# Three accumulation banks in attention and one buffer set in the quantization of a two-layer transformer kernel

## The chip, the cores and the metric

The kernel runs on 8 cores of one Trainium2 chip. Each core works on one of 8 sequences (2048 tokens by 1024 features), all with the same program and without exchange between them. The metric is the time on the device of the slowest core, in microseconds (us).

## The reference, cut to what matters

Two transformer layers, each an attention and a feed-forward block on a layer-normalized input, each added to x. All data is float32.

```python
x = x + L0_attn(layernorm(x))     # 16 heads of 64; causal; low-rank q, k, v; RMS norms on q and k
x = x + L0_ffn(layernorm(x))      # 1024 x 1024, ternary weights, activations rounded to 8 bits
x = x + L1_attn(layernorm(x))     # 16 heads of 64; causal; latent k and v
x = x + L1_ffn(layernorm(x))      # 1024 -> 4096 -> 1024

def L0_ffn(x, weight):
    w_scale = mean(abs(weight)) + 1e-8
    w_quant = clip(round(weight / w_scale), -1, 1)
    a_scale = max(abs(x), axis=-1, keepdims=True) + 1e-8
    a_quant = round(clip(x / a_scale * 127.0, -128.0, 127.0))
    return einsum('bsi,oi->bso', a_quant, w_quant) * (w_scale * a_scale / 127.0)
```

## The kernel before

**Stages.** x stays on the chip, transposed: eight tiles `X[c]` of 128 features by 2048 tokens. The stages follow one another with a barrier between them: entry (transposes), layer-0 attention `emit_l0a`, layer-0 feed-forward `emit_l0f`, layer-1 attention `emit_l1a`, layer-1 feed-forward, exit. The token axis is cut into four windows `qq` of 512 (`QW`).

**How the order comes about.** Every instruction is written by `do(engine, build, r=..., w=...)`. The five engines' queues run in the order in which the calls are written. From the names that an instruction reads (`r`) and writes (`w`) the helper works out what it waits for: a reader for the last writer of the name, a writer for the last writer and all readers. There are no other waits within a stage.

**Attention.** `attn_head` computes one head, in both layers, window by window. A window of queries has 4, 8, 12 or 16 blocks of 128 keys. Per block: the scores (L334, in the banks PS0, 1, 4 and 5 in turn), on the diagonal a mask added by a second matmul (L340), the exponential on ScalarE (L346, three tiles E32 in turn), and two blocks later the product with V (L352), which accumulates over the window in the bank `pvb`. That bank is PS2 in windows 0 and 2 and PS3 in windows 1 and 3. At the window's end ScalarE forms the reciprocal of the sums (L385 reads the bank, L388). The window's epilogue is held back and written after the fourth block of the next window, or at the start of the next pair of heads: TensorE moves the reciprocal to the other half of the partitions (L359, bank PS6), VectorE copies it (L363), multiplies the bank by it (L366, the last reader of the bank) and adds into X (L370). There are 2 layers of 8 pairs of heads, 4 windows a head, 128 windows in all. Ahead of each pair of heads TensorE makes its projections; in layer 0 they use the banks PS0 to PS7 (those of V, L627, PS2 and PS3; the norm sums PS6 and PS7), in layer 1 the banks PS2 to PS5, PS2 first. A prologue in layer 1 uses PS7 once.

**Quantization, in `emit_l0f`.** For each window the scale is spread over the partitions (L877, copied by L881 to RAB), and then for each of the eight chunks c of 128 features:
- GpSimd: XN = (X - MU) (L313), times RBC (L317), times RAB (L892);
- ScalarE: U = XN + 128.5 (L897), R = U (L901);
- VectorE, for k = 7 down to 0: B = (R >= 2^k) * 2^k (L906), R = R - B (L910), which leaves the fraction in R; then AQW[c] = U - 128 - R (L913), the rounded value.

The tiles XN, U, R and B are there twice and are taken in turn (in the trace `U__95`, `R__97`, `B__99`, `XN__101` are one set, `U`, `R`, `B`, `XN` the other). The matrix product L923 follows: eight output blocks of eight matmuls, each first block's matmul waiting for its chunk of AQW. VectorE scales each block's result (L938) and GpSimd adds it into X (L941); after that the next window begins.

Of the kernel before, what the change touches and what calls it, by code (L numbers as in the profile page):

```python
# [7 lines left out]
F32 = mybir.dt.float32  # L8
BF16 = mybir.dt.bfloat16
AF = mybir.ActivationFunctionType  # L10
OP = mybir.AluOpType
# [4 lines left out]
NCH = 8  # L16
NQ = 4
QW = 512
# [14 lines left out]
class KB:  # L33
# [286 lines left out]
    def attn_head(self, k_lhsT, kkey, q_rhs, qkey, v_lhsT, vkey, negc, nkey,  # L320
                  xout, xkey, half):
        s = self
        hs_ctx = slice(64, 128) if half else slice(0, 64)
        hs_z = slice(0, 64) if half else slice(64, 128)
        for qq in range(NQ):
            kcmax = 4 * qq + 4
            pvb = 2 + (qq % 2)
# [52 lines left out]
            if kcmax >= 2:  # L380
# [5 lines left out]
                 r=(f"PS{pvb}",), w=("TMPK",))  # L386
# [3 lines left out]
                 r=("TMPK",), w=("RBFz",))  # L390
# [293 lines left out]
    def emit_l0f(self):  # L684
        s = self
        WQ = s.ov("WQB", [128, 8 * 1024], BF16, 0)
        AQW = s.ov("AQW", [128, 8 * QW], BF16, 16 * 1024)
# [7 lines left out]
        UP = [s.ov("U_", [128, QW], F32, 62 * 1024),  # L695
              s.ov("U2", [128, QW], F32, 100 * 1024)]
        RP = [s.ov("R_", [128, QW], F32, 94 * 1024),
              s.ov("R2", [128, QW], F32, 102 * 1024)]
        BP = [s.ov("B_", [128, QW], F32, 96 * 1024),
              s.ov("B2", [128, QW], F32, 24 * 1024)]  # L700
        XNP = [s.ov("XN_", [128, QW], F32, 98 * 1024),
               s.ov("XN2", [128, QW], F32, 26 * 1024)]
        U_ = UP[0]
        XN_ = XNP[0]
# [16 lines left out]
        for m in range(2):  # L721
            for ch in range(8):
# [9 lines left out]
                 r=("PS2",), w=(f"AT{m}",))  # L732
# [142 lines left out]
        for qq in range(NQ):  # L875
# [6 lines left out]
            for c in range(NCH):  # L882
                p = (qq * NCH + c) % 2
                Ut, Rt, Bt, XNt = UP[p], RP[p], BP[p], XNP[p]
                uk, rk, bk_, xk = f"Up{p}", f"Rp{p}", f"Bp{p}", f"XNp{p}"
                wx = ("XN00", "XN01", "XN02", "XN03") if qq == 0 and c == 0 \
                    else ()
                if qq == 0 and c == 1:
                    wx = ("WPB",)
                s.xn_into(XNt[:], xk, c, qq, eng="gpsimd", wx=wx)  # L890
                s.do("gpsimd", lambda e, XNt=XNt, RAB=RAB:
                     e.tensor_tensor(XNt[:], XNt[:], RAB[:], OP.mult),  # L892
                     r=(xk, "RAB"), w=(xk,))
                uwx = ("XN10", "XN11", "XN12", "XN13") if qq == 0 and c == 0 \
                    else ()
                s.do("scalar", lambda e, Ut=Ut, XNt=XNt:
                     e.activation(Ut[:], XNt[:], AF.Identity,  # L897
                                  bias=s.SM[:, 30:31], scale=1.0),
                     r=(xk, "SM30"), w=(uk,) + uwx)
                s.do("scalar", lambda e, Rt=Rt, Ut=Ut:  # L900
                     e.activation(Rt[:], Ut[:], AF.Copy), r=(uk,), w=(rk,))  # L901
                for k in range(7, -1, -1):
                    val = float(1 << k)
                    kwx = ("WPB",) if qq == 0 and c == 1 and k == 7 else ()
                    s.do("vector", lambda e, val=val, Bt=Bt, Rt=Rt:
                         e.tensor_scalar(Bt[:], Rt[:], val, val, OP.is_ge,  # L906
                                         OP.mult),
                         r=(rk,), w=(bk_,) + kwx)
                    s.do("vector", lambda e, Rt=Rt, Bt=Bt:
                         e.tensor_tensor(Rt[:], Rt[:], Bt[:], OP.subtract),  # L910
                         r=(rk, bk_), w=(rk,))
                s.do("vector", lambda e, c=c, Ut=Ut, Rt=Rt, AQW=AQW:
                     e.scalar_tensor_tensor(  # L913
                         AQW[:, QW * c:QW * (c + 1)],
                         Ut[:], -128.0, Rt[:], OP.add, OP.subtract),
                     r=(uk, rk), w=(f"AQc{c}",))
# [580 lines left out]
```

How the kernel before makes its waits and increments, by code:

```python
        def f(e, build=build, real=tuple(real), sn_inc=sn_inc, n=n):  # L99
            for (sn, v0) in real:
                e.wait_ge(sems[sn], v0)
            build(e).then_inc(sems[sn_inc], n)
# [19 lines left out]
    def barrier(self):  # L122
        self.flush_ep()
        self.do("sync", lambda e: e.nop(),
                xw=[(sn, self.cnt[sn]) for sn in (*self.LDS, *self.STS)])
        vals = {}
        for e in ENGS:
            vals[e] = self.do(e, lambda en: en.nop(),
                              xw=[(ESEM[e], self.cnt[ESEM[e]])], force=True)
        for e in ENGS:
            for o in ENGS:
                if o == e:
                    continue
                sn = ESEM[o]
                if self.hw[e].get(sn, 0) < vals[o]:
                    self.hw[e][sn] = vals[o]
                    self.th[e].append(
                        lambda en, sn=sn, v0=vals[o]: en.wait_ge(self.sems[sn], v0))
            for sn in (*self.LDS, *self.STS):
                self.hw[e][sn] = max(self.hw[e].get(sn, 0), self.cnt[sn])
        self.floor = {ESEM[o]: vals[o] for o in ENGS}
        for sn in (*self.LDS, *self.STS):
            self.floor[sn] = self.cnt[sn]
```

## Time and profile before

| what | us |
|---|---|
| median of the timed runs (2) | 8110.35 |
| the two runs | 8074.76 and 8145.95 |
| the profiled execution | 7631.25 |
| its span on the slowest core | 7629.7 |
| spans of the eight cores | 7614.0 to 7629.7 |

Busy time in the profiled execution, on the slowest core:

| engine | busy us | share of the span | instructions |
|---|---|---|---|
| TensorE, matmuls (PE) | 5883.9 | 77% | 15346 |
| VectorE (DVE) | 2305.8 | 30% | 3740 |
| ScalarE (ACT) | 2055.3 | 27% | 3076 |
| GpSimd (POOL) | 618.5 | 8% | 580 |

The profile is of one execution, so durations and spans are to be compared with its own time and not with the median. Shares over the whole span are averages over stages that differ. "PEclk" is the granted TensorE clock as a share of 2.4 GHz. "Idle before" is time in which the engine stood still ahead of an instruction, put down to what released it last.

### The profile page before, as it was taken

Reading aid. Unit: us, or ns where it says so; the run is one execution under the profiler, and the core shown is the slowest. Engines: PE = TensorE matmul, PEld = TensorE weight load, DVE = VectorE, ACT = ScalarE, POOL = GpSimd, SP = SyncE. Lnnn points to the kernel's source line nnn. Section 1 sums busy time; section 2 is a strip of 40 time slices with the busy share of each in tenths; the row PEclk is TensorE's granted clock in tenths of the full one; section 3 lists DMA queues with packets and bytes.
Section 4 is the critical chain, followed back from the end, with each engine's and each line's share of the span. In section 5 each row is a group of like instructions: output and inputs, shape, how many; then the busy total and the mean of one; then the engine's idle time right before and its main releaser. Section 6 shows DMA issues by size and latency. Waiting matters only on the chain.

```text
span 7629.7 us, 101825 instructions; the slowest of 8 cores (7614.0 to 7629.7 us)
## 1 busy us (share of the span) xinstructions
PE 5883.9 (77%) x15346; PEld 2147.1 (28%) x15346; DVE 2305.8 (30%) x3740; ACT 2055.3 (27%) x3076; POOL 618.5 (8%) x580
## 2 busy tenths in 40 slices
PE   6888988889863112769878988898678879789786
PEld 2333333333321000222222222223223323223232
DVE  1333223332204677121111111111233332342323
ACT  1333333333310000103222322232342341432420
POOL 0000000000002332000000000000020120210200
PEclk8888998889975555889889989898889989999896
DMA  1000000000011000000000000000022222122221
GB/s 54 1 1 1 1 1 1 1 1 1 1 39 50 1 0 0 17 1 1 1 7 1 1 1 1 1 1 1 12 62 73 67 62 84 56 67 73 62 73 67
DMA packets 58437, 179.44 MB, mean 24 GB/s; under 512 B 9723, under 2 KB 16294, under 8 KB 57894
## 3 DMA queue, kind: packets, MB, share of 16 engines
q1 hardware_dynamic: 57894, 172.92, 7.4%
q8 instruction: 253, 4.15, 0.2%
q14 instruction: 290, 2.38, 0.1%
HBM read 164.44 MB, written 8.39 MB: 23 GB/s over the span
## 4 chain that ended last, share of the span: by engine, by line
PE 68%; DVE 15%; issue 8%; ACT 4%; DMA 2%; POOL 1%; DVEq 1%; ACTq 0%; SPq 0%; POOLq 0%; PEldq 0%
PE PS L334 16%; PE PS L352 15%; PE PS L1316 11%; PE PS L1252 7%; PE PS L340 2%; DVE W1L L1218 2%; PE PS L359 2%; ACT W1H L1216 1%; PE PS L279 1%; DVE R__97 L910 1%; PE PS L274 1%; DVE R L910 1%; PE PS L1001 1%; PE PS L1016 1%; PE PS L961 1%
## 5 line engine op out<-in xcount | busy, mean ns | idle before, releaser
L346 ACT ACTIVATE E<-PS,SM 128x512 f32<-128x512 f32 x1280 | 864.2, 686 | 1362.1 <-PE PS L340 684.4
L363 DVE COPY RBF<-PS 64x512 f32<-64x512 f32 x128 | 88.2, 689 | 2253.3 <-PE PS L359 2183.9
L334 PE MATMUL PS<-QP,KHD 64*128 64x512 f32 x1280 | 746.7, 675 | 10.8 <-issue 10.6
L352 PE MATMUL PS<-E,VFB 128*128 128x512 f32 x1280 | 659.7, 611 | 4.6 <-ACT E L346 4.6
L352 PE MATMUL PS<-E,VFA 128*128 128x512 f32 x1280 | 656.6, 611 | 1.3 <-ACT E L346 1.3
L1252 PE MATMUL PS<-XNH,W1H 128*128 128x512 bf16 x1024 | 434.9, 425 | 186.3 <-ACT W1H L1216 147.5
L1252 PE MATMUL PS<-XNH,W1L 128*128 128x512 bf16 x1024 | 436.2, 426 | 122.5 <-DVE W1L L1218 107.0
L1284 POOL TENSOR_TENSOR SC<-SC 128x512 f32<-128x512 f32 x128 | 161.6, 1263 | 3484.9 <-PE PS L1252 3454.1
L1252 PE MATMUL PS<-XNL,W1H 128*128 128x512 bf16 x1024 | 430.2, 420 | 0.3 <-DVE XNL L1200 0.2
L923 PE MATMUL PS<-AQW,WQB 128*128 128x512 bf16 x256 | 78.0, 445 | 455.8 <-DVE AQW L913 444.9
L1316 PE MATMUL PS<-ACH,W1H 128*128 128x512 bf16 x1024 | 388.8, 380 | 34.6 <-ACT ACH L1295 34.4
L1316 PE MATMUL PS<-ACL,W1H 128*128 128x512 bf16 x1024 | 388.8, 380 | 9.5 <-POOL ACL L1302 4.2
L1316 PE MATMUL PS<-ACH,W1L 128*128 128x512 bf16 x1024 | 388.7, 380 | 0.2
L334 PE MATMUL PS<-QA,KA 128*128 128x512 f32 x640 | 338.2, 623 | 0.0
L334 PEld LDWEIGHTS PS<-QP,KHD 64*128 64x128 f32 x1280 | 204.8, 196 | 471.7 <-issue 469.2
L1236 DVE TENSOR_TENSOR W1L<-W2F,W1H 128x1024 bf16<-128x1024 f32 x128 | 157.3, 1229 | 585.2 <-PE PS L1316 543.8
L334 PE MATMUL PS<-QB,KB 128*128 128x512 f32 x640 | 321.5, 596 | 0.0
L1233 ACT ACTIVATE W1H<-W2F 128x1024 bf16<-128x1024 f32 x128 | 135.1, 1055 | 671.7 <-PE PS L1316 671.7
L352 PEld LDWEIGHTS PS<-E,VFB 128*128 128x128 f32 x1280 | 231.2, 192 | 297.0 <-issue 290.7
L352 PEld LDWEIGHTS PS<-E,VFA 128*128 128x128 f32 x1280 | 232.3, 192 | 290.7 <-issue 284.3
L1218 DVE TENSOR_TENSOR W1L<-W1F,W1H 128x1024 bf16<-128x1024 f32 x127 | 177.2, 1395 | 316.5 <-ACT W1H L1216 267.1
L404 ACT ACTIVATE SC<-SC 128x2 f32<-128x2 f32 x32 | 6.5, 203 | 848.9 <-DVE SC L400 848.7
(243 smaller groups left out, 6823.6 us busy)
## 6 DMA issues: line engine op xcount, KB each, us to landing
W1F<-w1p SPq DMA_DIRECT2D x128, 512.0 KB, 3.7
W2F<-w SPq DMA_DIRECT2D x128, 512.0 KB, 3.6
TM<-x_in SPq DMA_DIRECT2D x16, 512.0 KB, 12.2
WTR<-w0T SPq DMA_DIRECT2D x16, 512.0 KB, 3.8
y_out<-XO SPq DMA_DIRECT2D x16, 512.0 KB, 2.6
WPA<-wo1T SPq DMA_DIRECT2D x16, 256.0 KB, 2.6
WPA<-wuq SPq DMA_DIRECT2D x8, 128.0 KB, 2.0
WPB<-wuk SPq DMA_DIRECT2D x8, 128.0 KB, 2.0
```

Of the source, the lines that this page charges most:

```text
L334: e.matmul(s.PS[sb][:], k_lhsT(kc), q_rhs(qq), start=True, stop=not diag),
L340: e.matmul(s.PS[sb][:], s.I128B[:], s.MSK[:, QW * j:QW * (j + 1)], start=False, stop=True),
L346: e.activation(s.E32[eb][:], s.PS[sb][:], AF.Exp, bias=negc),
L352: e.matmul(pvbank[:], v_lhsT(kc), s.E32[eb][:], start=(kc == 0), stop=(kc == kcmax - 1)),
L359: e.matmul(s.PS[6][hs_ctx, :], s.I128[hs_z, hs_z], s.RBF[hs_z, :], start=True, stop=True),
L910: e.tensor_tensor(Rt[:], Rt[:], Bt[:], OP.subtract),
L1218: e.tensor_tensor(w1l[:], w1f[:], w1h[:], OP.subtract),
L1233: e.activation(w2h[:, 0:1024], w2f[:], AF.Copy),
L1236: e.tensor_tensor(w2l[:, 0:1024], w2f[:], w2h[:, 0:1024], OP.subtract),
L1252: e.matmul(bank[:], lh[:, FCW * kc:FCW * (kc + 1)], rh[:, QW * kc:QW * (kc + 1)], start=(kc == 0 and pi == 0), stop=(kc == 7 and pi == 2)),
L1284: e.tensor_tensor(s.SC[0][:], s.SC[0][:], s.SC[3][:], OP.add),
L1316: e.matmul(s.PS[mch][:], lh[:, 128 * mch:128 * (mch + 1)], rh[:, QW * kc:QW * (kc + 1)], start=(kc == 0 and pi == 0), stop=(kc == 31 and p ...
```

## The change

Two edits. In `attn_head` the accumulation bank is taken from three, PS2, PS3 and PS7, by a counter that runs on over windows, heads and layers. In `emit_l0f` the second set of the tiles U, R, B and XN is dropped, and every chunk uses the one set under one set of names; the instructions themselves stay the same in kind, size, number and order.

```diff
         for qq in range(NQ):
             kcmax = 4 * qq + 4
-            pvb = 2 + (qq % 2)
+            s.pvc = getattr(s, "pvc", 0) + 1
+            pvb = (2, 3, 7)[s.pvc % 3]
             pvbank = s.PS[pvb]
...
-        UP = [s.ov("U_", [128, QW], F32, 62 * 1024),
-              s.ov("U2", [128, QW], F32, 100 * 1024)]
-        RP = [s.ov("R_", [128, QW], F32, 94 * 1024),
-              s.ov("R2", [128, QW], F32, 102 * 1024)]
-        BP = [s.ov("B_", [128, QW], F32, 96 * 1024),
-              s.ov("B2", [128, QW], F32, 24 * 1024)]
-        XNP = [s.ov("XN_", [128, QW], F32, 98 * 1024),
-               s.ov("XN2", [128, QW], F32, 26 * 1024)]
-        U_ = UP[0]
-        XN_ = XNP[0]
+        U_ = s.ov("U_", [128, QW], F32, 62 * 1024)
...
             for c in range(NCH):
-                p = (qq * NCH + c) % 2
-                Ut, Rt, Bt, XNt = UP[p], RP[p], BP[p], XNP[p]
-                uk, rk, bk_, xk = f"Up{p}", f"Rp{p}", f"Bp{p}", f"XNp{p}"
...
-                s.xn_into(XNt[:], xk, c, qq, eng="gpsimd", wx=wx)
+                s.xn_into(XN_[:], "XN", c, qq, eng="gpsimd", wx=wx)
...
-                s.do("scalar", lambda e, Ut=Ut, XNt=XNt:
-                     e.activation(Ut[:], XNt[:], AF.Identity,
+                s.do("scalar", lambda e, U_=U_, XN_=XN_:
+                     e.activation(U_[:], XN_[:], AF.Identity,
                                   bias=s.SM[:, 30:31], scale=1.0),
-                     r=(xk, "SM30"), w=(uk,) + uwx)
-                s.do("scalar", lambda e, Rt=Rt, Ut=Ut:
-                     e.activation(Rt[:], Ut[:], AF.Copy), r=(uk,), w=(rk,))
+                     r=("XN", "SM30"), w=("U",) + uwx)
+                s.do("scalar", lambda e, R_=R_, U_=U_:
+                     e.activation(R_[:], U_[:], AF.Copy), r=("U",), w=("R",))
                 for k in range(7, -1, -1):
                     val = float(1 << k)
...
-                         r=(rk,), w=(bk_,) + kwx)
+                         r=("R",), w=("B",))
...
-                         r=(rk, bk_), w=(rk,))
+                         r=("R", "B"), w=("R",))
...
-                     r=(uk, rk), w=(f"AQc{c}",))
+                     r=("U", "R"), w=(f"AQc{c}",))
```

## Rows read from the trace of the kernel before

**Rows 1.** Busy time by stage (from:to, length, engines' busy us, granted clock, DMA).
```profile
1000.00:2030.00 1030.00, 923.34 (x2108) 360.33 (x2107) 311.00 (x521) 376.12 (x581) 36.08 (x28) 0.89 0.00 1
...
2500.00:2900.00 400.00, 51.65 (x146) 16.35 (x146) 296.51 (x431) 32.44 (x48) 113.51 (x87) 0.53 0.00 0
...
3435.00:5380.00 1945.00, 1722.40 (x3648) 564.33 (x3647) 294.87 (x582) 555.56 (x831) 0.00 (x0) 0.90 0.00 1
...
5500.00:7520.00 2020.00, 1689.62 (x6124) 615.51 (x6122) 690.18 (x912) 634.36 (x895) 309.35 (x256) 0.92 0.22 67
```

**Rows 2.** TensorE's waits, whole run: line, releaser, us, times, longest.
```profile
PE PS L923 <- DVE AQW L913: 444.9, 31, 26.2
...
PE PS L352 <- ACT E L346: 5.9, 17, 1.3
...
PE PS L627 <- DVE TMPE L366: 2.9, 4, 0.9
```

**Rows 3.** Timeline over a border between heads: start, us, engine, line, operation.
```profile
363.83 1.07 PE L359 MATMUL PS<-RBF,I 64*64 64x512 f32 x2
...
365.94 0.68 DVE L366 TENSOR_TENSOR TMPE<-PS,RBF 64x512 f32<-64x512 f32 x1 [0.17 <-DVE RBF L363]
...
369.78 1.10 PE L352 MATMUL PS<-E,VFB 128*128 128x512 f32 x2 [0.39 <-ACT E L346]
```

**Rows 4.** Groups of the quantization, 2500 to 3060: count, busy, mean ns, idle before.
```profile
L910 DVE TENSOR_TENSOR R__97<-R__97,B__99 128x512 f32<-128x512 f32 x128 | 110.2, 861 | 13.3
...
L906 DVE TENSOR_SCALAR B__99<-R__97 128x512 f32<-128x512 f32 x128 | 81.4, 636 | 37.4 <-ACT R__97 L901 19.5 <-POOL XN L892 6.0
...
L897 ACT ACTIVATE U__95<-XN__101,SM 128x512 f32<-128x512 f32 x16 | 11.5, 722 | 617.9 <-POOL XN__101 L892 457.0 <-DVE AQW L913 160.9
```

**Rows 5.** Timeline of the first chunk of window 1.
```profile
2657.40 0.72 ACT L897 ACTIVATE U__95<-XN__101,SM 128x512 f32<-128x512 f32 x1 [47.79 <-POOL XN__101 L892]
2658.26 0.63 ACT L901 ACTIVATE R__97<-U__95 128x512 f32<-128x512 f32 x1
...
2659.07 1.10 DVE L906 TENSOR_SCALAR B__99<-R__97 128x512 f32<-128x512 f32 x1 [6.49 <-ACT R__97 L901]
...
2669.67 1.69 DVE L910 TENSOR_TENSOR R__97<-R__97,B__99 128x512 f32<-128x512 f32 x1
```

**Rows 6.** Timeline of the handover from that chunk to the next.
```profile
2676.85 0.69 DVE L913 SCALAR_TENSOR_TENSOR AQW<-U__95,R__97 128x512 bf16<-128x512 f32 x1 [0.17 <-DVE R__97 L910]
2677.46 0.42 DVE L906 TENSOR_SCALAR B<-R 128x512 f32<-128x512 f32 x1
2677.69 0.72 ACT L897 ACTIVATE U__95<-XN__101,SM 128x512 f32<-128x512 f32 x1 [14.58 <-DVE AQW L913]
...
2678.56 0.63 ACT L901 ACTIVATE R__97<-U__95 128x512 f32<-128x512 f32 x1
2678.61 1.27 POOL L313 TENSOR_TENSOR XN__101<-X,MU 128x512 f32<-128x512 f32 x1 [7.81 <-ACT U__95 L897]
2678.78 1.38 DVE L906 TENSOR_SCALAR B<-R 128x512 f32<-128x512 f32 x1
...
2680.27 1.63 DVE L910 TENSOR_TENSOR R<-R,B 128x512 f32<-128x512 f32 x1
2681.61 1.40 POOL L892 TENSOR_TENSOR XN__101<-XN__101,RAB 128x512 f32<-128x512 f32 x1 [0.27 <-POOL XN__101 L317]
...
2683.40 0.69 DVE L910 TENSOR_TENSOR R<-R,B 128x512 f32<-128x512 f32 x1
...
2690.91 0.69 DVE L913 SCALAR_TENSOR_TENSOR AQW<-U,R 128x512 bf16<-128x512 f32 x1 [0.17 <-DVE R L910]
```

**Rows 7.** VectorE's timeline: the last instruction of later chunks of window 1.
```profile
2733.11 0.69 DVE L913 SCALAR_TENSOR_TENSOR AQW<-U__95,R__97 128x512 bf16<-128x512 f32 x1 [0.17 <-DVE R__97 L910]
...
2744.41 0.69 DVE L913 SCALAR_TENSOR_TENSOR AQW<-U,R 128x512 bf16<-128x512 f32 x1 [0.17 <-DVE R L910]
...
2767.01 0.69 DVE L913 SCALAR_TENSOR_TENSOR AQW<-U,R 128x512 bf16<-128x512 f32 x1 [0.17 <-DVE R L910]
```

More of the change, by code:

```diff
@@ L882, in emit_l0f @@
             for c in range(NCH):
-                p = (qq * NCH + c) % 2
-                Ut, Rt, Bt, XNt = UP[p], RP[p], BP[p], XNP[p]
-                uk, rk, bk_, xk = f"Up{p}", f"Rp{p}", f"Bp{p}", f"XNp{p}"
                 wx = ("XN00", "XN01", "XN02", "XN03") if qq == 0 and c == 0 \
                     else ()
-                if qq == 0 and c == 1:
-                    wx = ("WPB",)
-                s.xn_into(XNt[:], xk, c, qq, eng="gpsimd", wx=wx)
-                s.do("gpsimd", lambda e, XNt=XNt, RAB=RAB:
-                     e.tensor_tensor(XNt[:], XNt[:], RAB[:], OP.mult),
-                     r=(xk, "RAB"), w=(xk,))
+                s.xn_into(XN_[:], "XN", c, qq, eng="gpsimd", wx=wx)
@@ L894, in emit_l0f @@
+                s.do("gpsimd", lambda e, XN_=XN_, RAB=RAB:
+                     e.tensor_tensor(XN_[:], XN_[:], RAB[:], OP.mult),
+                     r=("XN", "RAB"), w=("XN",))
                 uwx = ("XN10", "XN11", "XN12", "XN13") if qq == 0 and c == 0 \
                     else ()
-                s.do("scalar", lambda e, Ut=Ut, XNt=XNt:
-                     e.activation(Ut[:], XNt[:], AF.Identity,
+                s.do("scalar", lambda e, U_=U_, XN_=XN_:
+                     e.activation(U_[:], XN_[:], AF.Identity,
@@ L898, in emit_l0f @@
                                   bias=s.SM[:, 30:31], scale=1.0),
-                     r=(xk, "SM30"), w=(uk,) + uwx)
-                s.do("scalar", lambda e, Rt=Rt, Ut=Ut:
-                     e.activation(Rt[:], Ut[:], AF.Copy), r=(uk,), w=(rk,))
+                     r=("XN", "SM30"), w=("U",) + uwx)
+                s.do("scalar", lambda e, R_=R_, U_=U_:
+                     e.activation(R_[:], U_[:], AF.Copy), r=("U",), w=("R",))
                 for k in range(7, -1, -1):
                     val = float(1 << k)
[L904 to L907, printed above, removed]
-                         r=(rk,), w=(bk_,) + kwx)
-                    s.do("vector", lambda e, Rt=Rt, Bt=Bt:
-                         e.tensor_tensor(Rt[:], Rt[:], Bt[:], OP.subtract),
-                         r=(rk, bk_), w=(rk,))
@@ L912, in emit_l0f @@
-                s.do("vector", lambda e, c=c, Ut=Ut, Rt=Rt, AQW=AQW:
+                    s.do("vector", lambda e, val=val, B_=B_, R_=R_:
+                         e.tensor_scalar(B_[:], R_[:], val, val, OP.is_ge, OP.mult),
+                         r=("R",), w=("B",))
+                    s.do("vector", lambda e, R_=R_, B_=B_:
+                         e.tensor_tensor(R_[:], R_[:], B_[:], OP.subtract),
+                         r=("R", "B"), w=("R",))
+                s.do("vector", lambda e, c=c, U_=U_, R_=R_, AQW=AQW:
@@ L913, in emit_l0f @@
                      e.scalar_tensor_tensor(
                          AQW[:, QW * c:QW * (c + 1)],
-                         Ut[:], -128.0, Rt[:], OP.add, OP.subtract),
-                     r=(uk, rk), w=(f"AQc{c}",))
+                         U_[:], -128.0, R_[:], OP.add, OP.subtract),
+                     r=("U", "R"), w=(f"AQc{c}",))
             for mch in range(NCH):
```

## The prediction

> **What bounds the kernel now.** I read the table of stages first, to see which engine sets the pace in the two places that the change touches. In both attention stages TensorE is busy for 90% of the time (923 of 1030 us of the first, 1722 of 1945 us of the second) at a mean granted clock of 0.89 and 0.90; in the quantization the picture is reversed: VectorE is busy for 297 of 400 us, TensorE for 52, at a granted clock of 0.53 [rows 1]. The same is seen from TensorE's list of waits: its largest is the one of L923 for the quantized activations of L913, 444.9 us in 31 waits, while the product with V (L352), the only instruction that takes a new accumulation bank in attention, was idle for 5.9 us over the whole run, and for the scores' exponentials, not for a bank [rows 2]. So the first attention stages are TensorE's own speed, and the quantization is a chain of VectorE. The timelines then give the chain's price chunk by chunk [rows 5 to 7], and the group list says how many such chunks there are: 16 on the buffer set shown and as many on the other, 32 in all, with 8 comparisons (L906) and 8 subtractions (L910) each [rows 4].
>
> **The change, edit one: three accumulation banks.** With two banks, a window's first L352 may start only when L366, the last reader of the window two before, is through. The tightest place is a short first window of a head, since only four key blocks stand between. There L366 starts at 365.94 and takes 0.68, so it is done at 366.62; the bank's next first L352 starts at 369.78, after 0.39 us idle for an exponential [rows 3]. The bank had been free for 3.2 us. A third bank moves a release that is already early. Its gain is at least 0 and at most what the list shows on L352 and on the V projections that wait for L366: 5.9 + 2.9 = 8.8 us [rows 2]. Against it, bank 7 is also used by the norm sums of layer 0, and at three of the seven borders between head pairs of layer 1 the pending bank is now bank 2, the first that the projections want. TensorE would then wait for the two VectorE steps of 0.68 us, about 1.5 us a time [rows 3], so under 5 us for all three; in layer 0 these steps precede the norm sums on VectorE's own queue in any case. I take 0 for this edit, bounds -9 and +5.
>
> **Edit two: one buffer set instead of two in the quantization.** No instruction is removed or added. What goes is that ScalarE's two copies of the next chunk (L897, then L901) could run before VectorE had finished the present one. L897 writes U, which L913 reads last, and L901 writes R, which the subtractions work in, so both now stand between one chunk and the next. The handover is read off the timeline, T being the start of L913 at 2676.85 [rows 6].
> - Now: the next chunk's first comparison starts at 2677.46, T + 0.61.
> - After: L897 starts after L913, as the one shown does, at 2677.69 or T + 0.84; L901 at 2678.56 or T + 1.71, ends 0.63 later at T + 2.34; VectorE starts 0.18 after such an end (2658.26 + 0.63 = 2658.89 to 2659.07 [rows 5]), so at T + 2.52.
> - The bare gap grows by 2.52 - 0.61 = 1.91 us. There are 7 handovers in a window and 4 windows; the first chunk of a window has both copies in front of it already [rows 5].
>
> That would be 28 x 1.91 = 53.5 us. But GpSimd's part has to be followed too. It normalizes a later chunk with three instructions (L313, L317, L892), from 2678.61 to 2681.61 + 1.40 = 2683.01, and VectorE's instructions beside them are long: a comparison takes 1.38 where one later takes 0.43, a subtraction 1.63 where one takes 0.69 [rows 6]. The period from L913 to L913 is 14.06 us with GpSimd beside it (2676.85 to 2690.91 [rows 6]) and 11.30 without (2733.11 to 2744.41; 2744.41 to 2767.01 is two of the same [rows 7]): 2.76 us for one chunk's normalization.
>
> Where does it fall now? With two buffers GpSimd runs ahead. During a window's first chunk VectorE is slowed without a break from 2659.07 to the end of the subtraction of 2669.67. An undisturbed chunk takes 11.30 - 0.61 = 10.69 us from its first comparison to L913; this one took 2676.85 - 2659.07 = 17.78, so 7.09 more [rows 5, 6]. Four chunks of 14.06 follow up to 2733.11, then three of 11.30 up to 2767.01 [rows 7]. The sum checks: 17.78 + 56.24 + 33.90 = 107.92, against 2767.01 - 2659.07 = 107.94 us, of which 7.09 + 4 x 2.76 = 18.1 us is lost beside GpSimd.
>
> With one buffer, GpSimd may start on the chunk after the next only when L897 has read XN, 0.2 us after L897's end, so at T + 1.76 as in the shown handover. So each of the first seven chunks has one normalization beside it. It starts 0.76 us before VectorE's first comparison. In the shown handover a comparison that met the first L313 ended at 2678.78 + 1.38, T + 3.31, wherever it had begun; I take that end for the first comparison of the new chunk. Of the 16 comparisons and subtractions 15 then remain, where 13 remained in the shown handover, which took 10.75 us from T + 3.31 to T + 14.06. The two more are one undisturbed pair, 10.69 / 8 = 1.34 us, so 12.09 us, and the period is 15.40, against 11.30 + 1.91 = 13.21 for a chunk with nothing beside it: a normalization costs 2.19 instead of 2.76, because part of it lies under ScalarE's copies.
>
> A window afterwards: first chunk 10.69 + 2.19 = 12.88, six of 15.40 = 92.40, the last 13.21, together 118.49 us. Before 107.94. That is 10.55 us a window, four windows: **+42 us**. The matrix products behind the chain (L923) wait for its last chunk in both kernels, and GpSimd's additions into X stand ahead of the next window's normalization in both, so nothing of it is covered by the window's tail.
>
> The Trainium skill, page "SBUF — State Buffer", section on the two separate sides, says that VectorE (with two SBUF inputs) and GpSimd take their shared port as an exclusive lock, the loser blocking for the whole instruction. The rows agree: a 0.69 us subtraction became 1.63 [rows 6]. By this rule the first comparison ends as I took it, and the sum is 42 us; if the loss were shared in proportion to the overlap instead, 2.76 x (4.40 - 0.76) / 4.40 = 2.28 us would be lost, and the sum would be 4 x (7 x 1.91 + 7 x 2.28 - 18.1) = 45 us.
>
> Bounds where the trace can't show the new overlap: if no normalization disturbed VectorE any more, 4 x (7 x 1.91 - 18.1) = -19 us; if each cost its full 2.76, 4 x (7 x 1.91 + 7 x 2.76 - 18.1) = +58 us. I stay at 42, since the shown handover has the same start of L313.
>
> **The sum.** The profiled execution took 7631 us; by it the new kernel takes 7631 + 42 = 7673, 0.55% more. The median of the timed runs, 8110, lies 479 us above the profiled one and the two runs differ by 71 us. The added time is VectorE's and ScalarE's, which TensorE's clock doesn't stretch, so I add the same 42 us to the median: **8152 us**. About 2% (162 us) is what a measurement of this kernel can tell from no change, so this is "within 2%".
>
> **The rivals.**
> - *The banks pay back the buffers* (not slower than before): edit one gains 42 us or more, 8110 us or less. It would need 0.33 us in each of the 128 windows, hidden in the matmuls' own durations. Against it stands the 3.2 us by which the bank was early [rows 3]. Chance 0.07.
> - *The ring was worth nothing*: less overlap with GpSimd gives back the gaps, -19 to +15 us, 8091 to 8125. For it: 18.1 us a window is lost beside GpSimd now. Against it: the three instructions remain, and start only 0.76 us before VectorE. Chance 0.05.
> - *GpSimd falls out of its cover*: the normalization starts only after VectorE's chain. It would add 4.40 + 0.3 us to each of the 28 periods of 13.21 while the disturbance goes: a window of 10.69 + 7 x 17.9 = 136 us, 28 us more, +112 in all, 8222 us. It decides only if something but L897 holds XN; the code names no other reader. Chance 0.06.
> - *TensorE's clock falls* (slower by over 2%): place, both attention stages; there TensorE is busy about 3,400 us at a mean grant of 0.9, seen as part of the time at 2.4 GHz and part at less [rows 1]. A mean lower by 0.05 costs 3,400 x 0.05 / 0.9 = 189 us, 8341 in all; with the 42 us it passes 2% from a fall of 0.03. Nothing in the rows ties the grant to the choice of bank. The Trainium skill, page "TensorE: Matmul & The Clock Gate", section on a second failure mode by cycling through PSUM banks, describes TensorE losing its clock by small idle times when it moves from bank to bank; the kernel before moves between two banks already, and the rows show almost no idle time at L352. Chance 0.05.
> - *The clock is granted more freely in the runs of the new kernel*, for reasons outside the change: under 7948 us. The 479 us between profiled and timed executions show that such differences exist. Chance 0.03.
>
> **How the numbers follow.** The forecast has 0.74. Its own range is 8150 plus or minus some 60 us (the bounds of edit two and half the distance of the two runs shown). From 8060 to 8250 the range takes in the rivals of the banks, of the ring and of GpSimd, and leaves out the two of the clock and the tails of the runs' scatter, 0.08 and some 0.12, together 2 in 10. Faster by over 2%: 0.03 for the clock and 0.01 for the banks, 0.04. Slower by over 2%: 0.05 for the clock and 0.01 for GpSimd's case in a slow sample, 0.06. Within 2%: 0.90.
>
> **What would show it.** In the new profile: L897 waits for L913 and L906 waits for L901, some 28 times; from the start of L913, L906 follows after 2.5 us instead of 0.6; periods of 15.4 us (six in a window) and one of 13.2; a window of 118 us instead of 108; TensorE's wait at L923 grows by about 42 us. L352's idle time stays below 10 us and the attention stages keep their length within 10 us. Wrong would be: attention stages shorter by tens of us at an equal grant (the banks mattered), periods of 17.9 us (GpSimd uncovered), or periods near 13 us in all chunks (the disturbance went away).

## The result, and the profile after

| | before | after |
|---|---|---|
| median of all timed executions, us | 7906.06 (14) | 8011.4 (17) |
| lowest and highest, us | 7627.82 to 8199.87 | 7696.35 to 8244.88 |
| spans of cores 4 to 7 in the profiled execution, us | 7614.0 to 7626.2 | 7687.5 to 7695.8 |

The ratio, after to before, is 1.0075 with a 95% interval of 1.0041 to 1.0109: slower by 0.75%, within 2%. In most executions of either kernel the granted TensorE clock is lower on some of the cores and the time grows by up to 8%, so the ratio is taken from executions in which it isn't, and the medians above can't be read against each other.

The forecast was 8152 us with a range of 8060 to 8250. The measured median lies 49 us below the range. The change in time that the prediction added, 42 us or 0.55%, lies inside the interval of the ratio, but that interval is wide (some 31 to 83 us), and the trace below has 67 us.

In the profiled execution of the changed kernel cores 0 and 1 took 7912.3 us and the other six 7687.5 to 7696.6. So everything below is read on core 6, and core 6 of the kernel before is beside it. The view of the cores:

```profile
core 0: 7912.3 us, clock 0.819
...
core 6: 7692.8 us, clock 0.851
```

Core 6 is 66.6 us longer than before (7692.8 against 7626.2). From the first or last start of the matmuls that mark each stage in the trace, in us:

| stretch on core 6 | before | after | difference |
|---|---|---|---|
| start to the first scale matmul of the quantization (L877; after: L869) | 2505.6 | 2504.4 | -1.2 |
| from there to the last start of L923 (after: L908) | 546.3 | 592.6 | +46.3 |
| to the first projection of layer 1 (L1001; after: L986) | 319.8 | 323.1 | +3.3 |
| to the last bound matmul of layer-1 attention (L407; after: L408) | 1909.2 | 1926.1 | +16.9 |
| to the end | 2345.3 | 2346.6 | +1.3 |

So two thirds came from the quantization, and a quarter from layer-1 attention, where the prediction had nothing. The first row is not as quiet as it looks: it hides 8.1 us that bank 7 costs just ahead of the quantization (shown under the experiments), because on this core the time up to the first bound matmul of layer-0 attention is 2.9 us shorter and that attention itself 4.9. The row differs from core to core, 2494.2 to 2507.4 us before and 2499.8 to 2510.8 on cores 4 to 7 after.

The list of TensorE's waits (releaser, us in total, times, longest) has both, the counterpart of [rows 2]:

```profile
PE PS L908 <- DVE AQW L898: 500.6, 32, 21.6
...
PE PS L986 <- DVE TMPE L367: 7.9, 3, 2.7
```

The wait for the quantized activations grew from 444.9 + 10.9 us (the second part stood before as a wait of L923 for L906) to 500.6. L353, the product with V, waits no less with three banks than with two (6.2 us in 17 waits, against 5.9 in 17). New are four waits for L367, the multiplication that frees an accumulation bank: three at the first projection of layer 1 (L986, in the list), and one of 2.0 us in the prologue (L1078).

**The handover in the quantization**, the counterpart of [rows 6], from the timeline of core 6, window 1:

```profile
2679.54 0.69 DVE L898 SCALAR_TENSOR_TENSOR AQW<-U__95,R__98 128x512 bf16<-128x512 f32 x1 [0.17 <-DVE R__98 L895]
2680.38 0.72 ACT L884 ACTIVATE U__95<-XN__100,SM 128x512 f32<-128x512 f32 x1 [13.89 <-DVE AQW L898]
...
2681.31 1.27 POOL L313 TENSOR_TENSOR XN__100<-X,MU 128x512 f32<-128x512 f32 x1 [10.99 <-ACT U__95 L884]
2682.05 0.80 DVE L892 TENSOR_SCALAR B__99<-R__98 128x512 f32<-128x512 f32 x1 [1.82 <-ACT R__98 L888]
```

VectorE restarts 2.51 us after the start of L898 (0.61 before). Its first comparison takes 0.80 and ends at T + 3.31, for it met GpSimd's L313, which had started 0.74 us earlier. The next two of its instructions, L895 and L892, are long as well, 1.63 and 1.30, and then the rest run at 0.43 and 0.69. Over the window, VectorE's timeline has these periods:

| us, window 1 | before | predicted | after |
|---|---|---|---|
| first comparison to L913 of the first chunk | 17.78 | 12.88 | 12.88 |
| next periods | 14.07 x 4, 11.30 x 3 | 15.40 x 6, 13.21 | 15.40 x 5, 15.75, 13.22 |
| window | 107.96 | 118.49 | 118.82 |

The four windows (0 to 3) grew by 11.0, 10.9, 10.9 and 11.2 us, 44.0 together. Window 0, which the prediction took to be like window 1, has some 0.9 us more in most of its periods, but in both kernels (12.20 for 11.30 before, 16.29 for 15.40 after). The other 2.3 us of the stage lie between the windows: the first comparison comes 0.3 us later after the scale copy in three of them.

**The border in layer-1 attention.** The same place in both kernels, between the first and the second pair of heads, core 6. Before, with bank 3 pending:

```profile
3621.09 3.78 PE L1001 MATMUL PS<-UU,WUQT 128*128 128x512 f32 x4
...
3622.20 0.69 DVE L366 TENSOR_TENSOR TMPE<-PS,RBF 64x512 f32<-64x512 f32 x1 [0.17 <-DVE RBF L363]
```

After, with bank 2 pending, the bank that the first projection writes:

```profile
3667.70 1.04 PE L360 MATMUL PS<-RBF,I 64*64 64x512 f32 x2 [1.99 <-ACT RBF L389]
...
3668.91 0.69 DVE L364 COPY RBF<-PS 64x512 f32<-64x512 f32 x1 [28.05 <-PE PS L360]
...
3669.78 0.69 DVE L367 TENSOR_TENSOR TMPE<-PS,RBF 64x512 f32<-64x512 f32 x1 [0.17 <-DVE RBF L364]
...
3671.36 3.45 PE L986 MATMUL PS<-UU,WUQT 128*128 128x512 f32 x4 [2.62 <-DVE TMPE L367]
```

Before, the projection followed its predecessor without a gap, and ran beside VectorE's L366. After, it stands still for 2.62 us: until L364 starts (0.17), L364 and L367 (0.69 each) with 0.18 between them, and 0.89 more from the end of L367 to the matmul.

### The profile page after: what moved, and what is told of

The parts are those of the page before. It is cut to its first block, busy times and chain, and to the rows that moved or that the text cites. A ratio compares the mean times of both kernels' runs of the same rounds, so it can differ in the third digit from the quotient of the medians.

```text
span 7912.3 us, 101841 instructions; the slowest of 8 cores (7687.5 to 7912.3 us)
## 1 busy us (share of the span) xinstructions
PE 6138.8 (78%) x15346; PEld 2227.0 (28%) x15346; DVE 2293.0 (29%) x3740; ACT 2061.2 (26%) x3076; POOL 614.9 (8%) x580
## 4 chain that ended last, share of the span: by engine, by line
PE 70%; DVE 14%; issue 8%; ACT 4%; DMA 2%; POOL 1%; DVEq 1%; ACTq 0%; SPq 0%; POOLq 0%; PEldq 0%
PE PS L335 17%; PE PS L353 16%; PE PS L1301 11%; PE PS L1237 7%; DVE R__98 L895 3%; PE PS L341 2%; DVE W1L L1203 2%; DVE B__99 L892 2%; PE PS L360 2%; PE PS L279 2%; ACT W1H L1201 1%; PE PS L274 1%; PE PS L986 1%; PE PS L1001 1%; PE PS L946 1%
## 5 line engine op out<-in xcount | busy, mean ns | idle before, releaser
L364 DVE COPY RBF<-PS 64x512 f32<-64x512 f32 x128 | 88.2, 689 | 2461.4 <-PE PS L360 2418.2
L353 PE MATMUL PS<-E,VFA 128*128 128x512 f32 x1280 | 711.1, 657 | 0.8 <-ACT E L347 0.8
L353 PE MATMUL PS<-E,VFB 128*128 128x512 f32 x1280 | 707.3, 651 | 2.7 <-ACT E L347 2.7
L1237 PE MATMUL PS<-XNH,W1L 128*128 128x512 bf16 x1024 | 435.2, 425 | 122.6 <-DVE W1L L1203 108.4
L908 PE MATMUL PS<-AQW,WQB 128*128 128x512 bf16 x256 | 79.4, 450 | 500.6 <-DVE AQW L898 500.5
L335 PE MATMUL PS<-QA,KA 128*128 128x512 f32 x640 | 389.8, 709 | 0.0
L335 PE MATMUL PS<-QB,KB 128*128 128x512 f32 x640 | 370.0, 676 | 0.0
L353 PEld LDWEIGHTS PS<-E,VFA 128*128 128x128 f32 x1280 | 252.4, 206 | 317.8 <-issue 310.2
L353 PEld LDWEIGHTS PS<-E,VFB 128*128 128x128 f32 x1280 | 248.1, 204 | 320.6 <-issue 312.8
L884 ACT ACTIVATE U__95<-XN__100,SM 128x512 f32<-128x512 f32 x32 | 23.1, 722 | 829.7 <-POOL XN__100 L879 433.6
```

The costliest lines, as they stand in the source:

```text
L335: e.matmul(s.PS[sb][:], k_lhsT(kc), q_rhs(qq), start=True, stop=not diag),
L353: e.matmul(pvbank[:], v_lhsT(kc), s.E32[eb][:], start=(kc == 0), stop=(kc == kcmax - 1)),
L1237: e.matmul(bank[:], lh[:, FCW * kc:FCW * (kc + 1)], rh[:, QW * kc:QW * (kc + 1)], start=(kc == 0 and pi == 0), stop=(kc == 7 and pi == 2)),
```

## The experiments

The short diffs are against the kernel before unless said otherwise. Lengths of spans and stages are read on undisturbed cores, which here means those whose span is not drawn out in that execution; each core is named.

### Each edit alone

Edit one alone (`e1_banks`, and a second time as `e11_banks_again`):

```diff
-            pvb = 2 + (qq % 2)
+            s.pvc = getattr(s, "pvc", 0) + 1
+            pvb = (2, 3, 7)[s.pvc % 3]
```

> The kernel before with edit one alone (three accumulation banks by the running counter). By the prediction: no change, -9 to +5 us. By the trace of the changed kernel: +11 us, all of it in layer-1 attention, 3.5 us at each of the three borders between head pairs where the pending bank is bank 2 (after the 1st, 4th and 7th pair), nothing at the other borders beyond some 3 us either way and nothing inside a head. Rival: the third bank costs or gains something in every window; then the time inside the heads differs as well.

> Edit one alone once more, for an interval. By the border waits 11 us, 0.15% more than before; by the spans of undisturbed cores in the first look (7642 to 7651 against 7614 to 7630) about 25 us, 0.3%. If it comes out above 0.2%, something beyond the three borders costs time.

Measured: layer-1 attention, from the first projection to the last bound matmul, takes 1919.2 us on core 2, 1925.9 on core 6, 1922.6 on core 7 of the first run and 1922.5 on core 0 of the second; before it is 1905.8 on core 5 and 1909.1 to 1909.3 on the others. That is +10 to +17 us, not the prediction's 0. From one bound matmul to the next, core 2 has +3.0, +3.7 and +3.9 us at the borders after the 1st, 4th and 7th pair and 0.0 to -0.5 at the other four; within pairs, never more than 0.4. Cores 3 and 6 have the same three (the last is 6.9 on core 6) and +2.5 once more inside a pair. So what repeats from core to core is the cost at the borders with bank 2 pending. The repetition gave a ratio of 1.0024 (0.9923 to 1.0125), too wide to say more; the first run gave no ratio with an interval. The spans of the undisturbed cores are 7642.2 to 7655.0 us against 7614.0 to 7629.7, so about 25 us, of which the three borders are some 11, and 8 more lie ahead of the quantization, as shown below.

Edit two alone (`e2_ring`): the diff of the quantization as in the change, `pvb` as before.

> The kernel before with edit two alone (one buffer set in the quantization). By the prediction: +42 us, periods of 15.4 us six times a window and 13.2 once, the attention stages unchanged. Rival: the two edits need each other for part of the cost; then edit two alone gives much less than the 42 to 47 us seen in the changed kernel's quantization.

Measured: ratio 1.0060 (1.0043 to 1.0077), 46 us. The quantization takes 591.5 us on core 0, 591.8 on core 6 and 594.0 on core 2, +45.2 to +47.7; window 1 takes 118.77 us with periods of 15.39 (five), 15.74 and 13.21. Layer-1 attention takes 1905.9 on core 6, 1909.2 on core 0 and 1912.7 on core 2, against 1905.8 to 1909.3 before. Edit two alone gives the whole growth of the quantization and no wait in attention: the edits don't need each other.

**What bank 7 costs ahead of the quantization.** Before the quantization, `emit_l0f` looks for the largest value of each token, in 16 rounds of eight transposes: four from tile XN into PS6 and four from tile U into PS7. The instructions of this line before and after, core 6, with first and last start:

```profile
L839 PE MATMUL PS<-I,XN__101 x64: 445/447/449, 2381.9 to 2494.8; 128*128 128x128 f32 x64
...
L839 PE MATMUL PS<-I,U__95 x64: 443/446/448, 2387.0 to 2496.2; 128*128 128x128 f32 x64
```

```profile
L831 PE MATMUL PS<-I,XN__100 x64: 445/447/448, 2372.7 to 2493.3; 128*128 128x128 f32 x64
...
L831 PE MATMUL PS<-I,U__95 x64: 445/447/448, 2377.9 to 2495.1; 128*128 128x128 f32 x64
```

From the first start to the last that is 114.3 us before and 122.4 after, 8.1 more, with each transpose as long as it was. On every core of every kernel here that keeps bank 7 out of the rotation it is 114.2 to 114.4 us, and on every core of every kernel that rotates over it 121.9 to 122.6, whatever the clock did on that core. In between, TensorE's queue (weight loads included) has 381 semaphore instructions before and 445 after: one more for each of the 64 transposes into PS7. The added one waits for ScalarE. The helper makes a writer wait for all engines that have ever read the name, and with bank 7 in the rotation ScalarE has read PS7 in attention (L386). That read is long over, so the wait is met, but it still takes time: from the first to the fourth transpose into PS7 of a round it is 1.06 us before and 1.37 after, and 8.1 / 64 is 0.13 us for each. No run took these waits away alone; their number and place speak for them. This is a cost of edit one that neither the prediction nor the list of waits has, since the list shows only waits that last.

### Which bank is pending at the border

Three banks, the last window of each pair always in bank 7 (`e3_bank7`):

```diff
-            pvb = 2 + (qq % 2)
+            pvb = (2, 3, 7)[(4 * half + qq + 1) % 3]
```

> Three banks as in edit one, but the count starts anew with each pair of heads, so that the last window of every pair accumulates in bank 7, which the next pair's projections do not use. If only the bank that is pending at the border counts: no wait of the projections for the multiplication by the reciprocal, and layer-1 attention as long as before (within 4 us). If three banks cost by themselves: +11 to +17 us as in the changed kernel.

Two banks, exchanged, so that the last window is always in bank 2 (`e4_bank2`):

```diff
-            pvb = 2 + (qq % 2)
+            pvb = 3 - (qq % 2)
```

> Two banks as before, but exchanged: the last window of each pair accumulates in bank 2, the first bank that the next pair's projections want. If the pending bank at the border is the cause: 7 borders of layer 1 at 3.5 us, +25 us, with 7 waits for the multiplication of 2.6 us each (18 us). If the third bank is the cause: no change.

TensorE's waits for the multiplication at the projections of layer 1, first of `e4_bank2`, core 6:

```profile
PE PS L1001 <- DVE TMPE L366: 13.2, 5, 2.7
```

(the sixth, of 2.7 us, stands in the list as a wait for L370), and of `e3_bank7`, core 6, where only the prologue of layer 1 waits, which uses bank 7:

```profile
PE PS L1093 <- DVE TMPE L366: 2.0, 1, 2.0
```

| | ratio to before | layer-1 attention, us |
|---|---|---|
| before | 1 | 1905.8 to 1909.3 |
| `e3_bank7` | 1.0007 (0.9993 to 1.0021) | 1902.1 to 1905.5 |
| edit one | see above | 1919.2 to 1925.9 |
| `e4_bank2` | 1.0044 (1.0029 to 1.0059) | 1943.2 |

In layer-1 attention three banks cost nothing when the pending bank is free of the next pair's use, and two banks cost 34 us when it is not. (The 7.6 us that bank 7 costs `e3_bank7` ahead of the quantization are within the interval of its ratio.) So at the border it isn't the third bank, it is bank 2. The size was missed: 34 us instead of 25. Six of the seven borders cost, +3.8, +3.6, +7.4, +4.1, +6.6 and +6.8 us on core 7, which is 5.4 on average; the border with the prologue in front costs nothing. What a border loses beyond its wait of 2.6 us is lost in the matmuls after it. In the changed kernel the keys' projection has a mean of 869 ns instead of 822, by the groups of layer-1 attention behind the first pair of heads on core 6, before and after:

```profile
L1016 PE MATMUL PS<-CKV,KEF 128*128 128x512 f32 x112 | 78.4, 822 | 54.3 <-issue 54.0
```

```profile
L1001 PE MATMUL PS<-CKV,KEF 128*128 128x512 f32 x112 | 82.8, 869 | 53.9 <-issue 53.7
```

**TensorE's clock in layer-1 attention.** The clock explains this, and more. In the traces of the cores below, the granted clock of this stage is always either 2.4 GHz or 1.2 GHz, and one matmul of the keys' projection takes 592 ns at the shortest and 1194 at the longest. The next table adds up, from the clock records of the trace, how long the stage stood at 1.2 GHz. Its last column takes half of that time off the length, an estimate of what the stage would take at the full clock:

| kernel, cores | waits for bank 2 | layer-1 attention, us | at 1.2 GHz, us | length less half of it |
|---|---|---|---|---|
| before, all | 0 | 1905.8 to 1909.3 | 404.6 to 414.9 | 1701.7 to 1703.5 |
| `e2_ring`, all | 0 | 1905.8 to 1912.7 | 408.1 to 425.2 | 1700.0 to 1701.8 |
| `e6_one_u`, all | 0 | 1912.6 to 1916.0 | 428.5 to 438.8 | 1696.6 to 1700.0 |
| `e3_bank7`, 4 to 7 | 0 | 1902.1 to 1905.5 | 397.6 to 407.8 | 1701.6 to 1703.3 |
| `e8_less` and `e12_less_again`, 4 to 7 | 0 | 1907.8 to 1919.1 | 417.0 to 445.3 | 1696.3 to 1699.3 |
| edit one, 0 to 3, 6 and 7, and 0 and 1 of the repetition | 3 | 1919.2 to 1925.9 | 424.9 to 438.5 | 1706.6 to 1708.3 |
| after, 4 to 7 | 3 | 1922.7 to 1926.1 | 431.8 to 438.6 | 1706.8 |
| `e4_bank2`, all | 6 | 1943.3 | 462.7 to 466.1 | 1710.2 to 1711.9 |

The last column orders the kernels by their waits: at most 1703.5 us with none, 1706.6 to 1708.3 with three, 1710.2 and more with six. On core 6 the change costs 5.0 us by it (1701.8 to 1706.8); a wait that falls into time at 1.2 GHz counts only half in this reckoning. The other 11.9 of the 16.9 us go with 23.7 us more at 1.2 GHz. Most of this time is not at the three borders. The largest piece on core 6 stands around the border after the third pair, where nothing waits for bank 2, before and after (start and end, length, busy us of TensorE, weight loads, VectorE, ScalarE and GpSimd, mean granted clock, DMA):

```profile
4052.00:4202.50 150.50, 126.25 (x285) 44.11 (x285) 26.94 (x59) 34.64 (x52) 0.00 (x0) 0.88 0.00 1
```

```profile
4103.50:4258.80 155.30, 130.56 (x284) 45.48 (x284) 26.91 (x59) 34.58 (x52) 0.00 (x0) 0.84 0.00 1
```

Whether edit one causes that share isn't shown: kernels without any wait for bank 2 spread over 397.6 to 445.3 us at 1.2 GHz, and over stage lengths of 1902.1 to 1919.1 us.

### Which buffer of the ring is the cost

One of the four tiles is single, the other three stay double (B was not tried alone). For XN (`e5_one_xn`); for U (`e6_one_u`) and R (`e7_one_r`) the index of that tile and of its name is 0 instead:

```diff
-                Ut, Rt, Bt, XNt = UP[p], RP[p], BP[p], XNP[p]
-                uk, rk, bk_, xk = f"Up{p}", f"Rp{p}", f"Bp{p}", f"XNp{p}"
+                Ut, Rt, Bt, XNt = UP[p], RP[p], BP[p], XNP[0]
+                uk, rk, bk_, xk = (f"Up{p}", f"Rp{p}",
+                                   f"Bp{p}", f"XNp{0}")
```

> The kernel before with one XN, but two of U, R and B. ScalarE can still run ahead of VectorE, so VectorE's next chunk starts 0.6 us after the start of the last instruction as before; the quantization keeps its length within 4 us. Rival: GpSimd's run ahead over two chunks is worth something by itself; then windows are longer by several us.

> The kernel before with one U, but two of XN, R and B. Both ScalarE copies stand between two chunks: VectorE restarts 2.52 us after the start of L913 instead of 0.61. Gaps 28 x 1.91 = 53 us, less what lies under the copies of the disturbance by GpSimd: +43 us, nearly the whole of edit two.

> The kernel before with one R, but two of XN, U and B. Only L901 stands between two chunks: VectorE restarts 0.84 + 0.63 + 0.18 = 1.65 us after the start of L913, 1.04 us later than before, and GpSimd starts after VectorE, so the disturbance keeps its 2.76 us: 28 x 1.04 = +29 us. Rival: the cost of the ring is that of GpSimd's normalization and not of ScalarE's copies; then one R costs nothing.

Read from VectorE's timeline in window 1, on core 4, core 6 and core 6. TensorE's clock differs between these executions (a mean of 0.799 to 0.853 on the cores read), but VectorE's steps don't show it: those that GpSimd doesn't disturb are 0.43 and 0.69 us in all of them.

| us | restart after the start of L913 | first chunk | periods beside GpSimd | others | window |
|---|---|---|---|---|---|
| before | 0.61 | 17.78 | 14.07 x 4 | 11.30 x 3 | 107.96 |
| one XN | 0.61 | 15.75 | 14.07 x 5 | 11.30 x 2 | 108.70 |
| one R | 1.59 | 17.77 | 14.97 x 4 | 12.29 x 3 | 114.51 |
| one U | 2.51 | 15.04 | 15.39 x 5 | 13.21, 13.22 | 118.43 (window 2) |
| all single (after) | 2.51 | 12.88 | 15.40 x 5, 15.75 | 13.22 | 118.82 |

One U costs 10.5 us a window, all but the whole of edit two (10.9); its quantization takes 588.4 us, +42.1. One XN costs 0.7 us a window: GpSimd's run ahead over two chunks is worth next to nothing, the disturbance only moves from the first chunk to a later one. One R costs 6.6 us, of which 7 x 0.98 = 6.9 are the later restart. It was expected at 1.65 and came at 1.59, as ScalarE's copy started 0.78 us after L913 here:

```profile
2763.20 0.69 DVE L914 SCALAR_TENSOR_TENSOR AQW<-U,R__97 128x512 bf16<-128x512 f32 x1 [0.17 <-DVE R__97 L911]
2763.98 0.63 ACT L902 ACTIVATE R__97<-U__95 128x512 f32<-128x512 f32 x1 [13.72 <-DVE AQW L914]
```

The costs are not additive: U and R single do not cost 10.5 + 6.6, since R's copy is written behind U's in ScalarE's queue anyway.

### What GpSimd's normalization takes from VectorE

`e9_one_norm`, against edit two alone; the two multiplications are left out:

```diff
-                s.xn_into(XN_[:], "XN", c, qq, eng="gpsimd", wx=wx)
-                s.do("gpsimd", lambda e, XN_=XN_, RAB=RAB:
-                     e.tensor_tensor(XN_[:], XN_[:], RAB[:], OP.mult),
-                     r=("XN", "RAB"), w=("XN",))
+                s.do("gpsimd", lambda e, c=c, qq=qq, XN_=XN_:
+                     e.tensor_tensor(XN_[:], s.X[c][:, QW * qq:QW * (qq + 1)],
+                                     s.MU[:, QW * qq:QW * (qq + 1)],
+                                     OP.subtract),
+                     r=(f"X{c}q{qq}", f"MU{qq}"), w=("XN", *wx))
```

> The kernel with edit two alone, but GpSimd only subtracts the mean; its two multiplications per chunk (L317 and L892) are left out, so the activations are not scaled. This measures the disturbance. If VectorE is held up for GpSimd's instructions: 28 normalizations lose some 1.7 us each, and the start of each window 2 x 1.47, so the quantization is about 60 us shorter than with edit two alone. If GpSimd's instructions cost VectorE nothing, only the four starts count: about 12 us shorter.

VectorE's comparisons and subtractions in the quantization, by groups, of edit two alone and then of `e9_one_norm`, core 0 of both (count, busy us, mean ns, idle before):

```profile
L894 DVE TENSOR_TENSOR R__98<-R__98,B__99 128x512 f32<-128x512 f32 x256 | 202.9, 793 | 28.4 <-DVE B__99 L891 2.3
L891 DVE TENSOR_SCALAR B__99<-R__98 128x512 f32<-128x512 f32 x256 | 142.2, 556 | 102.1 <-ACT R__98 L887 70.2 <-POOL XN__100 L317 6.0 <-ACTq L128 1.8
```

```profile
L895 DVE TENSOR_TENSOR R__98<-R__98,B__99 128x512 f32<-128x512 f32 x256 | 177.2, 692 | 27.4 <-DVE B__99 L892 0.9
L892 DVE TENSOR_SCALAR B__99<-R__98 128x512 f32<-128x512 f32 x256 | 118.8, 464 | 87.3 <-ACT R__98 L888 60.6 <-ACTq L128 1.8 <-DVE R__98 L895 0.9
```

Without GpSimd's two multiplications the subtractions are back at 692 ns, the undisturbed value, and the two kinds together are 202.9 + 142.2 - 177.2 - 118.8 = 49.1 us less busy. The period in window 1 is 13.59 us instead of 15.39, 1.8 us for two instructions, and the window 105.85 instead of 118.77. The quantization takes 524.3 us on core 0, 67 us less than edit two alone (591.5 on its core 0); expected were 60. Of the 67 us, 49 are the disturbance; most of the rest is that each window's first chunk is ready sooner. So VectorE's long instructions come from GpSimd's work beside them.

### A version meant to beat both

`e8_less`, `e12_less_again` (the same) and `e10_quant` (the same with the banks of before). The core of it:

```diff
-            s.do("vector", lambda e, RAB=RAB:
-                 e.tensor_copy(RAB[:], s.PS[6][:]), r=("PS6",), w=("RAB",))
+            s.do("vector", lambda e, RAB=RAB, qq=qq:
+                 e.tensor_tensor(RAB[:], s.PS[6][:],
+                                 s.RBC[:, QW * qq:QW * (qq + 1)], OP.mult),
+                 r=("PS6", f"RB{qq}"), w=("RAB",))
...
-                s.do("scalar", lambda e, Rt=Rt, Ut=Ut:
-                     e.activation(Rt[:], Ut[:], AF.Copy), r=(uk,), w=(rk,))
                 for k in range(7, -1, -1):
+                    St, sk = (Ut, uk) if k == 7 else (Rt, rk)
```

The comparison and the subtraction read `St` where they read `Rt`, and GpSimd's multiplication by RBC falls away.

> A version meant to beat both: two buffer sets as before; the last window of every pair in bank 7; RBC is multiplied into RAB once per window (in place of the copy of the bank to RAB), so that GpSimd has two instructions per chunk instead of three; and the first comparison and subtraction read U directly, so that ScalarE's copy to R falls away. If GpSimd's instructions hold VectorE up as before: the disturbance falls from 18.1 to about 12 us a window, the window's start by 1.5 + 0.8 us, together 4 x 8.4 = about 33 us less than before. If the disturbance is not what makes the chunks long: 9 us less.

> The faster quantization alone (scale multiplied into RAB once per window, no copy to R), with the accumulation banks of the kernel before. On undisturbed cores the quantization is 30 us shorter than before, as with the version that also rotates the banks, and attention is as long as before: about 0.4% less in all. If the rotation with bank 7 last contributed something, this one is slower than that version by as much.

> The version meant to beat both once more, for an interval: 0.4% less than before by the quantization (30 us), 0.2% by the spans of the undisturbed cores in the first look (7603 to 7613 us).

| us, undisturbed cores | before | with bank 7 last | banks of before |
|---|---|---|---|
| quantization | 546.1 to 546.8 | 515.7 to 517.4 | 515.3 to 516.0 |
| window 1 | 107.96 | 102.33 | 102.33 |
| span | 7614.0 to 7629.7 | 7590.4 to 7613.3 | 7586.8 and 7594.9 |

The quantization is 30 us shorter in every run (33 were expected); the periods are 13.25 x 4 and 11.30 x 3 and the first chunk 15.40. The rotation adds nothing to it. It costs the version with bank 7 last the 8 us ahead of the quantization, and its layer-1 attention is 1907.8 to 1919.1 us against 1905.8 to 1909.3, with more time at 1.2 GHz and no wait for bank 2 (the table above). By these readings the version with the banks of before is the better one. The spans of undisturbed cores are some 10 to 35 us shorter, and the lowest timed execution of `e10_quant` is 7604.4 against 7625.4 of the kernel before on the same chip. But no ratio with an interval came of it. So: shorter by 30 us in the stage, and in all likelihood by 0.2 to 0.4% in all, which the timed runs don't prove.

## Why the prediction was right or wrong, point by point

- **The base, the step that failed.** The forecast added the 42 us to 8110 us, the median of two executions, with a range set by half their distance. Over 14 executions the same kernel's median is 7906, over a range of 7628 to 8200. The base was 204 us too high, five times the effect. On the right base the same sum gives 7906 + 42 = 7948; the measured 8011 lies between that and the forecast, and below the range. The prediction saw that the profiled execution stood 479 us below and still took two executions 71 us apart for a spread. Both lay in the upper part of the 14, the profiled one at their bottom. A range from the profiled execution to the timed ones would have been the honest one.
- **What bounds the kernel**: right. Attention is TensorE's, the quantization VectorE's chain.
- **Edit two, +42 us**: right in mechanism and size; measured +46.3 with both edits and +45.2 to +47.7 alone. The gap (2.52 us predicted, 2.51 measured), the first comparison's end (T + 3.31, the same), the period (15.40, 15.40) and the first chunk (12.88, 12.88) were right. What was missing: one or two periods in each of windows 1 to 3 are longer by some 0.35 us (why was not looked into), and 2.3 us fall between the windows, the largest piece (1.1) behind the third.
- **The disturbance by GpSimd**: right, and shown by `e9_one_norm`. The lock that the Trainium skill describes, page "SBUF — State Buffer", section on the two separate sides, agrees with a comparison that ends at T + 3.31 wherever it began, 0.80 us long here and 1.38 before. The rival of a loss shared in proportion, +45 us, is nearer to the measured sum, but it misses the single period (15.49 by its figures against 15.40).
- **Edit one, 0 us, bounds -9 to +5, the second step that failed**: the side without gain was right; L352 and L353 wait alike, and the third bank brings nothing. The size was wrong: layer-1 attention grows by 13 to 17 us in the changed kernel, where the prediction had it within 10. The three borders had been named, and priced at 1.5 us each from VectorE's two steps alone. Each wait is 2.6 us, for 0.17 + 0.18 + 0.89 us lie between the steps, and what a border costs with the projections after it is 3.3 to 3.9 us. The trace before could not give the 0.89: there the V projections of layer 0, which wait for L366 too, start 0.36 to 0.39 us after its end. Two uses of bank 7 were overlooked. The prologue's wait (2.0 us) cost nothing, since the stretch around it is no longer than before. The transposes for the row maxima cost 8.1 us, by waits that are already met. So edit one costs 8 us there and, at the three borders, 5 us by the estimate at full clock and 11 us as measured.
- **What stays open.** Three borders make 10.6 us of the 13 to 17 in layer-1 attention. The rest of it, the 3.3 us in the stretch before it, and the 3.0 in the one from its last bound matmul to the first matmul of layer 1's feed-forward block have no wait to their name. They go with time at 1.2 GHz: on core 6 it grew from 83.4 to 93.9 us in the stretch before and from 53.2 to 59.7 in the one behind. Both pieces also appear with the banks of before: 323.0 us for the stretch before on core 1 of `e2_ring`, and +3.0 to +3.9 us for the one behind with `e2_ring` and `e10_quant`. Why the clock falls at one place in one kernel and not in the next is open.
- **The rivals.** The banks did not pay back (a cost of 13 to 17 us, not a gain). The ring was not free (+46). GpSimd kept its cover: periods of 15.4 and not 17.9. TensorE's clock did not fall by the 0.03 that this rival needed: the mean over the span is 0.851 after against 0.853 before on core 6. But in layer-1 attention it fell from 0.891 to 0.886, and some 12 us go with that. (The 3,400 us in that rival's price don't come out of [rows 1], whose two stretches have 2,646; the trace has some 3,490 in both stages.)
- **The chances**: within 2% was given 0.90, and came. That the added 42 us lie inside the measured interval is in part luck: edit two's share was right, and edit one's was missing.

## What to carry to other kernels

Before a second buffer is taken away, follow the chain that then stands in one queue: here the one tile that ScalarE wrote first, U, carried nearly the whole cost, and GpSimd's XN none. When accumulation banks are rotated, look at which bank is pending where the next phase begins, and at the bank that this phase asks for first; a running counter lets that vary, a fixed assignment can avoid it. Look also at what else uses the new bank: with a helper that waits for every engine that ever read a name, each later write into it pays for one more wait. And take the base of a forecast with its spread: edit two was forecast to 4 us here, and the kernel's own time missed by 200.

## What the runs showed of the hardware that was not expected

- A wait that has long been met is not free on TensorE's queue: with 64 more of them the transposes for the row maxima took 7.6 to 8.1 us longer, 0.12 to 0.13 us for each.
- From the end of VectorE's read of a bank to the matmul that waited for it, 0.89 to 0.92 us passed at the first projection of layer 1, more than either VectorE step, but 0.25 us at the prologue's transpose and 0.36 to 0.39 at the V projections of layer 0. From TensorE's end to VectorE's start it was 0.17.
- Stages without any change in instructions or waits differ between kernels in steps. Bound matmul to bound matmul, cores 4 and 6 of the kernel before agree to 0.1 us over both attention stages, but with edit two alone layer-1 attention on core 6 has -1.2, +2.2 and -4.7 us at its first places and nothing above 0.6 us after the fourth. The same places have 4.7 us less, 4.8 more and 10.6 less time at 1.2 GHz. So a few us of a stage's length are no evidence for a cause until the time at 1.2 GHz has been counted.
- GpSimd's cost to VectorE depends on the start: three instructions of 1.26 to 1.40 us cost VectorE 2.76 us a chunk where they begin beside it (periods of 14.06 and 11.30), and 2.18 where they begin 0.74 us ahead (15.39 and 13.21).
